# A post-norm decoder layer on one core: expert rounds moved into the cross attention steps, head pairs on 64-row tiles, split weights by way of DRAM

## The chip, the cores and the metric

The kernel runs on one core of one Trainium2 chip. The metric is the device time of one execution in microseconds. The kernel before has a median of 1275.68 us over 3 runs (1275.11 to 1279.91).

Five engines work side by side, each through its own queue of instructions in order: TensorE (PE; its weight loads are listed apart as PEld), VectorE (DVE), ScalarE (ACT), GpSimd (POOL) and SyncE (SP), which here only issues DMAs. They wait for each other by semaphores.

## The reference

One decoder layer on x (2048 rows of 256) with a context of 1601 rows of 256:

```python
x = layernorm(x + linear_attention(x))            # 8 heads of 64; softmax over features for q, over rows for k
# cross attention: 16 heads of 16
scores = einsum('bhqd,bhkd->bhqk', Q, K) * scale
out    = einsum('bhqk,bhkd->bhqd', softmax(scores), V)
x = layernorm(x + out @ Wo + bo)
# feed-forward: 16 experts of 128, the best 4 of each row weighted, and one shared network
act  = silu(x @ w1[e].T) * (x @ w3[e].T)
x = layernorm(x + sum_e combine[:, e] * (act @ w2[e].T) + shared(x))
```

The kernel computes all 16 experts for all rows and multiplies the hidden vector by the gate (0 where the expert was not chosen).

## The kernel before, in words

**Rows, chunks, groups, steps.** The 2048 rows are 4 chunks of 512. Cross attention goes through 16 groups (4 chunks times 4 groups of 4 heads), and a group through KT = 13 steps, one for each 128 keys: 208 steps. In a step PE makes four score tiles (`scores`, L755: one head, 128 keys by 512 rows, into banks 0 to 2 in turn), ACT takes the exponential of each (L538), and `weigh` (L766) multiplies them by the values, four heads side by side in four 32-column strips of the array.

**Row maxima.** The exponentials need the maximum of each row and head first. PE makes the scores a second time, with rows on partitions (`max_unit`, L733, 400 keys a unit, 64 units a group, three banks), and DVE reduces each unit (`read_max`, L1084). This runs 16 steps ahead of the steps that use it (LEAD); a stretch of 79 units comes before the first step. The negated maximum is turned (`turn_max`), copied by ACT (`copy_max`, L487) and written by DMA into the query stack (`stack_max`), so that the score product subtracts it.

**Precision.** Scores are bf16 products: queries and keys are each split into three bf16 parts, and six products of parts are stacked on 96 of the 128 rows. The experts' products are fp32r with two parts each (x_hi, x_lo, w_hi, w_lo), three products: `hidden` (L902 to L904) has 12 matmuls of 512 columns a network, `second` (L917 to L921) has 6.

**Order.** Four stages follow each other: linear attention and projections, which end in the split of keys (DVE L997 to L1002) and queries (L1073 to L1077); the 79 units; the 208 steps, into which the end of each earlier chunk (turn, output projection, layernorm, gate logits) is placed at fixed steps; and the 68 expert rounds (4 chunks times 17 networks, index i), in which ACT and POOL also split the weights for the first 17 (`first_part_w`, `second_part_w` L405). A round on DVE is `silu` (L1246), gate times inner product (L1252), their product (L1260) and its second part (L1265); on ACT it is tanh (L575) and the first part (L582). All four DVE operations of a round are on DVE alone.

POOL clears the value array and writes the rows of ones into the key stack (L384 to L388) once the context product is done, and computes the inverse deviations (L394). SP issues the DMAs in a fixed order.

## Time and profile before

| | |
|---|---|
| median of 3 runs | 1275.68 us |
| the profiled execution | 1280.25 us, span 1278.4 us |
| PE, DVE, ACT, POOL busy | 92%, 72%, 49%, 8% of the span |
| first score tile of the steps | 293.7 us |
| last value product of the steps | 952.2 us |
| granted TensorE clock, mean | 0.956 of full speed |

```profile
PE   6993887799999999999999999999989989999996
PEld 3471555422323333333333332333227768888885
DVE  1317786697888878788887888878427767677675
ACT  1210222105777776777767777677783432322222
```

Each digit is the busy share of a fortieth of the span (32 us), in tenths. The steps of cross attention are digits 10 to 29: PE, DVE and ACT are all busy. The rounds of the experts are the last 10: PE is full and ACT is at a third of what it was.

### The profile page before, as it was taken

The numbers are of one execution on the slowest core, as the hardware profiler recorded it, in microseconds if no ns is written. First come the engines' busy times: TensorE is split into PE (matmuls) and PEld (weight loads), VectorE is DVE, ScalarE is ACT, GpSimd is POOL, SyncE is SP. The second block draws the span as 40 slices with busy tenths as digits, with TensorE's granted clock in tenths as the row PEclk, the third lists the DMA queues.
The fourth block names the chain that finished last, engine by engine and source line by source line (L and its number), as shares of the span: only waits on it lengthen the run. The fifth ranks groups of instructions, "written<-read, shape, count | busy, mean of one in ns | idle before, by whom it ended". The sixth has DMA issues, their size and how long they took to land. (4 is left out here: it accounts for less than half of the span.)

```text
span 1278.4 us, 16160 instructions
## 1 busy us (share of the span) xinstructions
PE 1177.9 (92%) x5844; PEld 579.3 (45%) x5844; DVE 925.0 (72%) x1830; ACT 628.3 (49%) x1141; POOL 107.4 (8%) x94
## 2 busy tenths in 40 slices
PE   6993887799999999999999999999989989999996
PEld 3471555422323333333333332333227768888885
DVE  1317786697888878788887888878427767677675
ACT  1210222105777776777767777677783432322222
POOL 1213011500000000000000000000013410000000
PEclk9997898857999999999999999999999989999998
DMA  8000962102000000000000000000004411212120
GB/s 294 1 1 33 139 73 74 50 0 62 14 13 2 13 14 13 1 14 13 14 8 7 14 14 14 1 2 1 1 4 153 132 50 59 83 50 83 51 83 17
DMA packets 43055, 53.13 MB, mean 42 GB/s; under 512 B 4864, under 2 KB 31168, under 8 KB 42720
## 3 DMA queue, kind: packets, MB, share of 16 engines
q1 hardware_dynamic: 39104, 48.55, 14.4%
q10 hardware_dynamic: 3872, 3.56, 0.9%
q8 instruction: 46, 0.75, 0.2%
q14 instruction: 33, 0.27, 0.1%
HBM read 44.06 MB, written 7.83 MB: 41 GB/s over the span
## 5 line engine op out<-in xcount | busy, mean ns | idle before, releaser
L1084 DVE TENSOR_REDUCE mpart<-psum 128x1 f32<-128x400 f32 (+1 forms) x1024 | 522.9, 567 | 105.8 <-PE psum L733 101.4
L538 ACT ACTIVATE region<-psum 128x512 f32<-128x512 f32 (+1 forms) x832 | 450.2, 598 | 183.5 <-PE psum L755 182.3
L733 PE MATMUL psum<-region 96*128 96x400 bf16 (+1 forms) x1024 | 308.8, 352 | 8.7 <-DVE mpart L1084 5.6
L755 PE MATMUL psum<-region 99*128 99x512 bf16 (+1 forms) x832 | 285.0, 386 | 12.6 <-DMA region<-maxT 9.7
L766 PE MATMUL psum<-region 128*32 128x512 f32 (+1 forms) x1664 | 223.4, 609 | 0.7 <-ACT region L538 0.7
L755 PEld LDWEIGHTS psum<-region 99*128 99x128 bf16 (+1 forms) x832 | 80.6, 100 | 236.1 <-ACT region L538 186.8
L733 PEld LDWEIGHTS psum<-region 96*128 96x128 bf16 x1024 | 101.3, 99 | 181.2 <-DVE mpart L1084 132.8
L582 ACT ACTIVATE act_hi<-act_h 128x512 fp32r<-128x512 f32 x68 | 43.0, 632 | 176.0 <-DVE act_h L1260 176.0
L902 PE MATMUL psum<-x_hi,w_hi 128*128 128x512 f32 x272 | 109.9, 404 | 1.9 <-POOL w_lo L405 1.9
L903 PE MATMUL psum<-x_lo,w_hi 128*128 128x512 f32 x272 | 108.0, 397 | 0.0
L904 PE MATMUL psum<-x_hi,w_lo 128*128 128x512 f32 x272 | 108.0, 397 | 0.0
L394 POOL TENSOR_TENSOR rstd<-var_eps,half_neg 128x1 f32<-128x1 f32 (+1 forms) x24 | 18.4, 767 | 863.8 <-DVE var_eps L1139 752.0
L1265 DVE TENSOR_TENSOR act_lo<-act_h,act_hi 128x512 fp32r<-128x512 f32 x68 | 48.8, 718 | 47.5 <-ACT act_hi L582 47.5
L1246 DVE SCALAR_TENSOR_TENSOR silu_h<-tanh_h,psum 128x512 f32<-128x512 f32 x68 | 46.6, 685 | 41.9 <-ACT tanh_h L575 41.8
L917 PE MATMUL psum<-act_hi,w_hi 128*128 128x512 f32 x136 | 54.6, 402 | 8.8 <-ACT act_hi L582 8.7
L1260 DVE TENSOR_TENSOR act_h<-silu_h,weighted 128x512 f32<-128x512 f32 x68 | 56.7, 834 | 2.3
L902 PEld LDWEIGHTS psum<-x_hi,w_hi 128*128 128x128 f32 x272 | 51.7, 190 | 14.0 <-POOL w_lo L405 2.2
L766 PEld LDWEIGHTS psum<-region 128*32 128x32 f32 (+1 forms) x1664 | 32.8, 108 | 54.9 <-ACT region L538 40.3
L904 PEld LDWEIGHTS psum<-x_hi,w_lo 128*128 128x128 f32 x272 | 51.4, 189 | 12.5
L575 ACT ACTIVATE tanh_h<-psum 128x512 f32<-128x512 f32 x68 | 40.4, 593 | 33.5 <-PE psum L904 33.5
L903 PEld LDWEIGHTS psum<-x_lo,w_hi 128*128 128x128 f32 x272 | 51.6, 190 | 11.4
L918 PE MATMUL psum<-act_hi,w_lo 128*128 128x512 f32 x136 | 54.7, 402 | 0.0
(148 smaller groups left out, 1027.0 us busy)
## 6 DMA issues: line engine op xcount, KB each, us to landing
blend_a<-gates_d SPq DMA_DIRECT2D x32, 256.0 KB, 3.2
blend_b<-gates_d SPq DMA_DIRECT2D x32, 256.0 KB, 3.2
region<-qparts_d SPq DMA_DIRECT2D x96, 64.0 KB, 2.2
region<-kparts_d SPq DMA_DIRECT2D x6, 800.5 KB, 28.0
qparts_d<-region SPq DMA_DIRECT2D x4, 768.0 KB, 3.5
kparts_d<-region SPq DMA_DIRECT2D x3, 800.5 KB, 5.3
xT<-in_xT SPq DMA_DIRECT2D x1, 2048.0 KB, 8.9
x_sb<-in_x ACTq DMA_DIRECT2D x1, 2048.0 KB, 24.1
```

Source lines behind the costliest of these rows:

```text
L538: act.activation(prob[0:r, s % 3, j, :], bank(n % ST_BANKS)[0:r], ACT.Exp).then_inc(p_ready, 1)
L733: pe.matmul(bank(MAX_BANKS[u % len(MAX_BANKS)])[:, 0:w], qstack[0:SROWS, buffer(G), j, qt * P:(qt + 1) * P], kstack[0:SROWS, g * GROUP + j ...
L755: pe.matmul(bank(n % ST_BANKS)[0:r], kstack[0:SROWS + LEVELS, g * GROUP + j, kt * P:kt * P + r], qstack[0:SROWS + LEVELS, buffer(G), j, :] ...
L766: mm = pe.matmul(bank(4)[VW * j:VW * (j + 1)], vals[0:r, kt, g * GROUP + j, :], prob[0:r, s % 3, j, :], start=(kt == 0), stop=(kt == KT - 1))
L902: pe.matmul(out_bank, w_hi[:, e, col], x2_hi[tok], start=(k == 0), stop=False)
L903: pe.matmul(out_bank, w_hi[:, e, col], x2_lo[tok], start=False, stop=False)
L904: mm = pe.matmul(out_bank, w_lo[:, e, col], x2_hi[tok], start=False, stop=(k == DK - 1))
L917: pe.matmul(bank(6 + d), w_hi[:, e, cols[d]], act_hi[:, i % 2, :], start=(e == 0), stop=False)
L918: pe.matmul(bank(6 + d), w_lo[:, e, cols[d]], act_hi[:, i % 2, :], start=False, stop=False)
L1084: dve.tensor_reduce(mpart[:, u // UNITS % 2, v // PIECES, v % PIECES:v % PIECES + 1], bank(MAX_BANKS[u % len(MAX_BANKS)])[:, 0:w], X, ALU. ...
L1260: dve.tensor_tensor(act_h[:, i % 2, :], silu_h[:, :], weighted[:, :], ALU.mult).then_inc(act_ready, 1)
L1265: dve.tensor_tensor(act_lo[:, i % 2, :], act_h[:, i % 2, :], act_hi[:, i % 2, :].bitcast(F32), ALU.subtract).then_inc(act_lo_ready, 1)
```

## The change

1. `max_unit` and `scores` take fp32r operands. Queries and keys have two parts each and three products, on 48 rows; two heads lie in the two 64-row halves of the array (side 0 and side 1). One max unit is now 512 keys of two heads in two banks, and DVE reduces both in one instruction of 1024 elements; 26 units a group, two a step, and two of the 26 hold the last 66 keys of four row tiles (8 short matmuls). LEAD is 17 steps. The maximum is not split any more.
2. 42 of the 68 rounds run inside steps 67 to 192, a third in each step: `part_of_round` makes six of the first inner products ("first"), the six matmuls of the round before's output ("out"), or the six of the second inner product ("second"). One bank (2) holds the inner product, banks 6 and 7 the output; the score ring shrinks from three banks to two, and the max units from two pairs of banks to one. The other 26 rounds follow the steps.
3. In these 42 rounds `product` and `second_part_act` are on POOL, and ACT takes the first part and tanh of a round between the second and third exponential of its "first" step.
4. Everything that used bank 5 (turns, projection, logits, gates) takes a slot of the score ring and is copied out by ACT; ACT's waits follow the ring.
5. `weigh` comes two steps behind (s - 2) and ahead of the step's scores; from step 67 on, scores 0 and 1 are adjacent, and 2 and 3.
6. The weights are split at the start: POOL makes both parts of each of the 17 networks, SP stores them to DRAM, and each round loads its own (768 KB) by one DMA. SP issues this before it stores the key parts; POOL does it before it clears the value array, and now fills the whole key stack with ones before the key loads.

```diff
-SPLIT = 6
-LEVELS = 3
+SPLIT = 3
+LEVELS = 2
...
+IN_STEPS = 42
+FIRST_PIECE = KT * GROUPS + KT + 2
...
+        def unit_bank(u):
+            return (4, 6)[u % 2] if u < SINGLE else 4
+        def unit_free(u):
+            return u - 1 if u < SINGLE else u
...
+        def ring_bank(n):
+            return n % 3 if n < NARROW else (n - NARROW) % 2
...
+            load_raw(0)
+            for e in range(FFN):
+                if e + 1 < FFN:
+                    load_raw(e + 1)
+                store_split(e)
+
             sp.wait_ge(k_split, 1)
...
+            for e in range(FFN):
+                pool.wait_ge(ld_raw[e % 2], 16 * 3 * (e // 2 + 1))
+                if e >= 2:
+                    pool.wait_ge(split_written[e % 2], 16 * (e // 2))
+                link(pool.tensor_copy(w_stage[:, e % 2, 0, :], w_raw[e % 2]))
+                pool.tensor_tensor(w_stage[:, e % 2, 1, :], w_raw[e % 2], w_stage[:, e % 2, 0, :].bitcast(F32),
+                                   ALU.subtract).then_inc(raw_split, 1)
...
-            pool.memset(region1[SROWS:SROWS + LEVELS, 0:KW], 1.0 + 0x3F80 * 2.0 ** -23).then_inc(zeros_ready, 1)
+            pool.memset(kstack[:, :, :].bitcast(F32), 1.0).then_inc(zeros_ready, 1)
...
+            def product(r):
+                pool.wait_ge(weighted_ready, r + 1)
+                if r >= 1:
+                    pool.wait_ge(act_lo_ready, r)
+                pool.tensor_tensor(act_h[0], silu_h[:, :], weighted[:, :], ALU.mult).then_inc(act_ready, 1)
...
                for j in range(GROUP):
+                    if j == 2:
+                        if kt == 1 and G >= 1:
+                            copy_num(G - 1)
+                        r, part = piece(s)
+                        if part == "first":
+                            if r >= 1:
+                                first_part_act(r - 1)
+                            tanh(r)
...
             def max_unit(u):
...
+                    for side in range(SIDES):
+                        rows_of = slice(HALF * side, HALF * side + SROWS)
+                        mm = pe.matmul(bank(unit_bank(u) + side)[:, at * w:(at + 1) * w],
+                                       qstack[rows_of, buffer(G), p, t * P:(t + 1) * P],
+                                       kstack[rows_of, g * PAIRS + p, keys], start=True, stop=True)
...
+            def part_of_round(s):
+                r, part = piece(s)
+                if part == "first":
+                    if r == 0:
+                        pe.wait_ge(ring_read, NARROW)
+                    else:
+                        pe.wait_ge(weighted_ready, r)
+                    inner(r, 0, bank(H_BANK))
+                if part == "out" and r >= 1:
+                    outer(r - 1)
+                if part == "second":
+                    pe.wait_ge(silu_ready, r + 1)
+                    inner(r, 1, bank(H_BANK))
...
             for s in range(STEPS):                           # PE
+                if s >= 2:
+                    weigh(s - 2)
+                scores(s, 0)
+                if s >= FIRST_PIECE:
+                    scores(s, 1)
                 for u in units[0:1]:
                     max_unit(u)
+                part_of_round(s)
+                if s < FIRST_PIECE:
+                    scores(s, 1)
+                scores(s, 2)
+                if s >= FIRST_PIECE:
+                    scores(s, 3)
+                for u in units[1:]:
                     max_unit(u)
+                if s < FIRST_PIECE:
+                    scores(s, 3)
+                behind_scores(s)
...
+                for u in range(units_until(s - 1), units_until(s)):
+                    read_max(u)
+                    if u % UNITS == UNITS - 1:
+                        finish_max(u // UNITS)
+                r, part = piece(s)
+                if part == "first":
+                    silu(r)
+                if part == "second":
+                    weigh_inner(r)
```

## Rows read from the trace of the kernel before

**Rows 1.** Windows by stage: length; PE, PEld, DVE, ACT, POOL busy; clock; DMA share; GB/s.

```profile
294.00:910.00 616.00, 601.59 (x3498) 200.91 (x3496) 508.85 (x1101) 439.79 (x817) 10.72 (x9) 0.99 0.04 12
910.00:952.00 42.00, 36.74 (x207) 8.37 (x206) 9.10 (x40) 34.43 (x68) 0.00 (x0) 0.96 0.01 1
952.00:1031.00 79.00, 68.11 (x302) 53.01 (x299) 55.70 (x91) 32.06 (x53) 33.60 (x19) 0.95 0.41 120
1031.00:1278.00 247.00, 236.57 (x1028) 190.28 (x1026) 171.22 (x281) 71.39 (x121) 5.88 (x5) 0.98 0.19 60
```

**Rows 2.** Timeline of PE in one attention step: start, duration, what.

```profile
502.96 1.07 PE L766 MATMUL psum<-region 65*32 65x512 f32 x8
503.96 0.39 PE L755 MATMUL psum<-region 99*128 99x512 bf16 x1
504.19 0.68 PE L733 MATMUL psum<-region 96*128 96x400 bf16 x3
...
505.95 0.64 PE L766 MATMUL psum<-region 128*32 128x512 f32 x4
```

**Rows 3.** Groups by shape, 400 to 800 us: busy, mean ns; idle before.

```profile
L538 ACT ACTIVATE region<-psum 128x512 f32<-128x512 f32 x460 | 249.7, 599 | 106.1 <-PE psum L755 105.7
L1084 DVE TENSOR_REDUCE mpart<-psum 128x1 f32<-128x400 f32 x462 | 244.8, 567 | 52.8 <-PE psum L733 51.2
```

**Rows 4.** Timeline of PE and ACT in the last steps, where no maxima are left.

```profile
941.90 1.07 PE L766 MATMUL psum<-region 128*32 128x512 f32 x8
...
944.30 0.64 PE L766 MATMUL psum<-region 128*32 128x512 f32 x4
...
940.93 2.06 ACT L538 ACTIVATE region<-psum 128x512 f32<-128x512 f32 x4 [0.33 <-PE psum L755]
```

**Rows 5.** Timeline of PE in the expert rounds and at their end.

```profile
1035.40 0.62 PE L921 MATMUL psum<-act_lo,w_hi 128*128 128x512 f32 x2
1035.85 0.40 PE L902 MATMUL psum<-x_hi,w_hi 128*128 128x512 f32 x1
...
1039.58 0.62 PE L921 MATMUL psum<-act_lo,w_hi 128*128 128x512 f32 x2
...
1266.45 0.62 PE L921 MATMUL psum<-act_lo,w_hi 128*128 128x512 f32 x2
```

**Rows 6.** Groups by shape, 1040 to 1200 us, of DVE and ACT.

```profile
L1246 DVE SCALAR_TENSOR_TENSOR silu_h<-tanh_h,psum 128x512 f32<-128x512 f32 x38 | 26.1, 686 | 17.1 <-ACT tanh_h L575 17.1
L582 ACT ACTIVATE act_hi<-act_h 128x512 fp32r<-128x512 f32 x38 | 24.0, 632 | 92.6 <-DVE act_h L1260 92.6
```

**Rows 7.** Timeline of PE: gate logits and output projection of a chunk.

```profile
523.30 1.85 PE L822 MATMUL psum<-gate_wT,attnT 128*128 128x16 f32 x16
...
976.86 1.89 PE L800 MATMUL psum<-wo_c,attnT 128*128 128x256 f32 x8
```

**Rows 8.** GpSimd: timeline rows, and L400 from the groups of 400 to 800 us.

```profile
28.85 10.98 POOL L381 TENSOR_TENSOR x_sb<-x_sb,bo_row 128x256 f32<-128x256 f32 x16 [26.16 <-DMA gate_wT<-in_gateT]
97.96 10.77 POOL L388 MEMSET region<- 3x12808 f32 x1
965.73 1.83 POOL L405 TENSOR_TENSOR w_lo<-w_raw,w_hi 128x768 fp32r<-128x768 f32 x1 [4.79 <-ACT w_hi L522]
L400 POOL TENSOR_TENSOR x_lo<-attnT,x_hi 128x512 fp32r<-128x512 f32 x4 | 5.1, 1278 | 61.0 <-ACT x_hi L509 61.0
```

**Rows 9.** Timeline of DVE: first and second key part operation, and the next one.

```profile
100.61 8.97 DVE L997 TENSOR_SCALAR region<-region 128x1601 f32<-128x1601 f32 x1
...
110.65 1.82 DVE L999 TENSOR_TENSOR region<-region 128x1601 f32<-128x1601 f32 x1
...
132.12 0.69 DVE L1045 TENSOR_REDUCE small<-psum 128x8 f32<-128x512 f32 x1 [7.88 <-DMA kparts_d<-region]
```

**Rows 10.** DMA issues: count, KB each, us from issue to landing.

```profile
kparts_d<-region SPq DMA_DIRECT2D x3, 800.5 KB, 5.3
```

More of the change, by code:

```diff
@@ L61, in buffer @@
     return (G + 1) % GROUPS
[L64 to L70 removed]
+assert LASTK > 0 and REST * TPC <= CHUNK and UNITS == PER_STEP * KT
 def decoder_layer(nc, a, out):
@@ new lines, in ffn_copy_step @@
+        def ffn_copy_step(c):
+            step = FIRST_PIECE + 3 * FFN * (c + 1) + 2
+            return step if FFN * (c + 1) < IN_STEPS else None
+        EXTRA = {}
+        for group in range(CHUNKS * GROUPS - 1):
+            EXTRA[KT * group + TURN_MAX_AT] = ("max", group + 1)
+            EXTRA[KT * (group + 1) + 2] = ("num", group)
+        for c in range(CHUNKS - 1):
+            first = CHUNK_STEPS * (c + 1)
+            jobs = [(4, "attnT", 0), (5, "attnT", 1), (6, "proj", 0), (7, "proj", 1), (KT - 2, "x2T", 0),
+                    (KT - 1, "x2T", 1), (KT, "logits", 0), (KT + 4, "gate", 0)]
+            if ffn_copy_step(c) is not None:
+                jobs += [(ffn_copy_step(c) + 3 + half - first, "ffn", half) for half in range(2)]
+            for at, what, which in jobs:
+                assert first + at not in EXTRA
+                EXTRA[first + at] = (what, (c, which))
@@ new lines, in copy_ffn, with tanh @@
+                if c >= 1:
+                    if ffn_copy_step(c - 1) is not None:
+                        act.wait_ge(ring_full, extra_slot("ffn", (c - 1, 1)) + 1)
+                    else:
+                        act.wait_ge(ffnN_ready, 2)
+                for d in range(DK):
+                    act.activation(ffnT[:, d, :], bank(O_BANK + d), ACT.Copy).then_inc(ffn_copied, 1)
+            def tanh(r):
+                act.wait_ge(h1_ready, r + 1)
+                if r >= 1:
+                    act.wait_ge(silu_ready, before(r))
+                b = H_BANK if r < IN_STEPS else 2 * place(r)
+                act.activation(tanh_h[:, place(r), :], bank(b), ACT.Tanh, scale=0.5).then_inc(tanh_ready, 1)
@@ new lines, in outer @@
+            def outer(r):
+                c, i = divmod(r, FFN)
+                w_hi, w_lo = weights(r)
+                if r == 0:
+                    pe.wait_ge(max_read, SINGLE)
+                if i == 0 and c >= 1:
+                    pe.wait_ge(ffn_copied, DK * c)
+                pe.wait_ge(act_hi_ready, r + 1)
+                cols = [slice(2 * DK * HID + d * P, 2 * DK * HID + (d + 1) * P) for d in range(DK)]
+                for d in range(DK):
+                    pe.matmul(bank(O_BANK + d), w_hi[:, cols[d]], act_hi[place(r)], start=(i == 0), stop=False)
+                    pe.matmul(bank(O_BANK + d), w_lo[:, cols[d]], act_hi[place(r)], start=False, stop=False)
+                pe.wait_ge(act_lo_ready, r + 1)
+                for d in range(DK):
+                    mm = pe.matmul(bank(O_BANK + d), w_hi[:, cols[d]], act_lo[place(r)],
+                                   start=False, stop=(i == FFN - 1))
+                mm.then_inc(act_done, 1)
```

1235 lines of the change are left out of this document (697 added, 538 removed).

## The prediction

> **What bounds the kernel now.** I read the windows by stage first, then one step of each stage on the timeline. The attention steps take 616 us for steps 0 to 191 and 42 us for the last 16, the expert rounds 79 + 247 us [rows 1]. A round costs 4.18 us, 18 matmuls at 0.23 us with no gap [rows 5], so this stage is PE's. An attention step takes 2.99 us from one value product to the next; the value product holds PE 1.00 us, a score 0.23 us [rows 2]. Four scores and 4.9 units of 400 columns (about 0.17 us each, three recorded as 0.68 us with 0.34 us for the last to drain) give 2.7 us: PE is close to its limit, with about 0.3 us lost to handshakes. ACT and DVE are idle for 106 and 53 us of 400 there [rows 3]. With group and chunk ends a step averages 616 / 192 = 3.21 us; without maxima it is 2.40 us [rows 4]. So a round is moved from a stage where PE alone works to one where PE has little room: the matmuls stay on the bound engine, and the change gains only if the steps' own PE work shrinks, or waits get filled.
>
> **The terms.** All are made against the profiled span, 1278.4 us.
>
> Head, before the first score. The key split falls from 12 DVE operations to 4; the first half had cost 15 us with a first scale of 8.97 us while GpSimd filled the ones [rows 8, 9]. I put the split's end about 13 us earlier; its store grows from 2.4 to 3.2 MB, so the 7.9 us wait [rows 9] becomes 10.5. Against this stands SP's queue: the key store stands behind 17 weight stores, and these behind GpSimd. GpSimd is free at 39.8 us; a subtraction of 768 columns takes 1.83 us [rows 8], the copy I put at 1.3 us, between 0.7 and 1.8. With two slots and loads of 4 to 5 us a network takes 3.9 us (3.2 to 4.5), so the last is split at 106 us (94 to 116), just ahead of the keys at 111. If that cover is gone, each us more is a us lost. The fill of ones (10.8 us) then falls beside DVE's work from 112 us on and may hold one DVE operation for up to 8 us as it did before. Query split and first maxima: some 7 us less. Together -14 us, between -25 and +8.
>
> Steps 0 to 66. Before: 67 x 3.21 = 215 us. After, DVE has 24 reads of 1024 elements a group. I take 1.18 us each from 0.57 us for 400 [rows 3] at the same slope, so 2.3 us a step; ACT has 2.06 us [rows 4] plus 0.12; PE has 1.00 plus 8 matmuls, of which those on opposite halves may overlap: 5 to 8 times 0.23 gives 2.2 to 2.9 us. With 0.25 us of handshake I take 2.55 us, 171 in all, plus about 20 for ends of groups and of chunk 0: 191 us, -24.
>
> **Steps 67 to 192, the core.** Before: 125 x 3.21 + 2.6 = 404 us. After, PE has per step: value product 1.00, two score pairs and two unit pairs at 0.25 each if the halves overlap, six matmuls of a round 1.40, two more changes between the full array and halves 0.14 (the value product loses 0.15 to its two changes: 8 records of two passes of 512 columns in four strips are 0.85 us of streaming). That is 3.54 us. The short units are set by weight loads, 16 in 1.85 us [rows 7], so 0.9 us in place of 0.25 twice a group: 3.64 us on average, 10.9 us a round.
>
> Waits come on top. In the "second" step the last unit is read by DVE (1.2 us) ahead of `weigh_inner` (0.69), and PE's next "first" part waits for that: 0.6 us. Then the product on GpSimd (1.28 us, [rows 8]), the first part (0.63, [rows 6]) and tanh run in a row ahead of the third exponential; this ends 5.75 us into the step, and scores 0 and 1 of the next step need its bank in the ring of two: 0.8 us. A round is then 12.4 us; 42 are 521 us. Behind the delayed exponentials stand ACT's copies and the value product two steps on, which has slack. Twenty turns of groups take 0.6 us each plus 0.5 waiting for a ring bank: 22. Two chunk ends: 8 slots each, 8.4 us of PE (projection 1.89 each, logits 1.85, [rows 7]), 4 us of waiting, 6 us in which DVE is in norms and gate choice and PE waits at the next unit, since there is one pair of banks: 37. Two ends of expert chunks: 10. Sum 590 us, 4.68 a step: +186. From 490 (every wait filled) to 650.
>
> SP stands in order behind the round's waits; the 768 KB load is issued in the "out" step and needed two steps later, 7 us; a transfer of 800 KB took 5.3 us [rows 10]. I cost it at nothing; with the cover gone it is 1 to 2 us a round.
>
> Steps 193 to 207: two ring banks and no round. Score, exponential and 1.00 us of value product follow each other: 2.9 us (2.4 to 3.1) against 2.6: +5.
>
> **Tail.** Before 326 us. After: 26 rounds x 4.18 = 109, the end of chunk 3 on PE 9, one pair of turns 1, waits for DVE 6, last output 2, and from the last matmul to the end 11.5 as now (1266.9 to 1278.4, [rows 5]): 138.5, -188 (-195 to -175). The first 13 rounds had taken 75 us in place of 54, partly for weight splits that are gone.
>
> Sum: 1278.4 - 14 - 24 + 186 + 5 - 188 = 1243 us of span, 1245 with the 1.9 us around it, against 1280.25. The median of the kernel before is 0.9964 of that: **1241 us**, 2.7% less.
>
> **The row that carries it.** No row shows row tiles. The nearest is the value product, four column strips: one record of 256 columns over the full array takes 0.236 us (1.89 / 8, [rows 7]), so eight of 512 would take some 3.4 to 3.8 us one by one, and take 1.00 [rows 2]: strips overlap at 85% or better. For the two halves I take the same. The bounds are 0.23 and 0.47 us a pair.
>
> The Trainium skill, "TensorE: Matmul & The Clock Gate", Part 3, says that tiles in different row groups run side by side and measured 3.07 times for four; by it a pair would be between 0.23 and 0.30 us and the sum at most 25 us higher. Its "TensorEngine Tiling (Array Packing)", Key Properties, speaks against this change: a switch of tiling mode drains TensorE. The value product agrees in kind; a step now has four switches for two, and by a drain of twice what I take the sum would be 18 us higher.
>
> **Rivals.**
> - *The halves do not overlap.* Steps 67 to 192 get 0.88 us more PE work each, which fills some of the waits: 13.8 us a round, +57; steps 0 to 66 go to 3.1 us, +37. About 1334 us, slower by 4.6%. For: different halves are a form no row shows, and each score raises a semaphore and waits for its own bank, so pairs can come apart. Against: the strips. It decides once a mean step from 67 to 192 is above 4.96 us.
> - *DVE and PE in lockstep.* From step 67 a unit may only be written when the one before was read. DVE's other work (silu and `weigh_inner` 0.46 us a step, norms and gates another 0.5) then shows on PE. I count about 20 of 120 us; with half of it 1290 us, slower by 1.1%. For: DVE waits in order for tanh in "first" steps. Against: PE has 1.4 to 1.7 us of other work between two units.
> - *The waits are filled.* GpSimd and ACT finish in time, scores are not held: 1.4 us x 42 and half of the ends' waits go, about 1162 us. For: ACT is idle for 27% of 400 us now [rows 3]. Against: the chain through GpSimd above.
>
> **How the numbers follow.** Forecast 0.45 (1205 to 1275), waits filled 0.20 (1140 to 1205), lockstep 0.17 (1275 to 1310), no overlap 0.18 (1300 to 1350). The measurement tells 0.5% from no change, so 1269 to 1282 is "same". Faster: 0.42 + 0.20 = 0.62. Same: 0.03 + 0.05 = 0.08. Slower: 0.12 + 0.18 = 0.30. The range takes most of the outer cases and the head's bounds: 1165 to 1325.
>
> **What would show it.** Right: a score pair whose two matmuls start within 0.05 us and a pair period near 0.25; 12.4 us between "first" parts, with 0.6 and 0.8 us idle for `weigh_inner` and for the ring; steps 67 to 192 in 590 us; first score near 280; about 138 us after the last value product. Wrong: pairs 0.47 apart; PE waiting for reads of maxima in most steps; SP behind `act_done` with PE waiting for weights; or key stores that wait for GpSimd's splits.

## The result, and the profile after

| | before | after |
|---|---|---|
| median of 4 runs (range), us | 1277.8 (1275.1 to 1280.5) | 1291.3 (1288.3 to 1291.9) |
| span of the profiled execution, us | 1278.4 | 1289.7 |
| first score, us into the span | 293.7 | 266.7 |
| tail behind the attention steps, us | 326 | 136 |

The ratio is 1.0105, with a 95% interval of 1.0084 to 1.0126: the changed kernel is 1.05% slower, where 1241 us was forecast. Executions that are over 1.5% slower than the fastest of their kernel, at a lower granted clock, are left out of every ratio and of every difference below. The windows of the changed kernel by stage (columns as in [rows 1]), from the first units of maxima to the last value product:

```profile
229.00:267.00 38.00, 27.19 (x85) 11.20 (x85) 36.75 (x35) 0.59 (x1) 0.00 (x0) 0.54 0.06 19
267.00:476.00 209.00, 202.04 (x1212) 86.40 (x1211) 162.34 (x166) 150.80 (x293) 3.57 (x3) 0.92 0.06 18
476.00:1083.00 607.00, 556.11 (x3068) 269.36 (x3066) 390.59 (x489) 346.81 (x645) 114.85 (x90) 0.97 0.24 76
1083.00:1154.00 71.00, 58.85 (x205) 16.21 (x205) 0.85 (x3) 35.11 (x65) 1.27 (x1) 0.56 0.21 83
```

The stages against the forecast, whose total was 1243 us of span:

| stage | forecast | measured |
|---|---|---|
| head, to the first score | 280 | 267 |
| steps 0 to 66 | 191 | 209 |
| steps 67 to 192 (rounds inside) | 590 | 607 |
| steps 193 to 207 | 44 | 71 |
| tail | 138.5 | 136 |

The tail came as forecast. The miss of 46 us is -13 + 18 + 17 + 27 - 3, in four places. The windows are cut at the first matmul of a round, at 476 us; the value product that begins step 67 starts at 473.1 and that of step 193 at 1084.2. By the starts of steps, as all sums of steps below are made, it is 206 us for steps 0 to 66 and 611 for steps 67 to 192. The row of steps 193 to 207 shows the largest miss: a granted clock of 0.56, against 0.96 for the last steps in [rows 1].

One quiet step with a third of a round in it, TensorE's timeline (start, duration, what; "x2" is a head pair):

```profile
1054.64 1.06 PE L1034 MATMUL psum<-region 128*32 128x512 f32 x8
1055.63 0.50 PE L1023 MATMUL psum<-qstack,kstack 49*128 49x512 f32 x2
1056.03 0.50 PE L996 MATMUL psum<-kstack,qstack 48*128 48x512 f32 x2
1056.46 0.50 PE L1180 MATMUL psum<-x_hi,w_slots 128*128 128x512 f32 x1
...
1058.05 0.51 PE L1023 MATMUL psum<-qstack,kstack 49*128 49x512 f32 x2
1058.39 0.39 PE L996 MATMUL psum<-kstack,qstack 48*128 48x512 f32 x2
1058.71 0.64 PE L1034 MATMUL psum<-region 128*32 128x512 f32 x4
```

There is no gap. From start to start: value product 0.99 us, the pairs 0.40, 0.43, 0.34 and 0.32, six matmuls of the round 1.59, in all 4.07. The forecast for the same step was 3.54 and some waits. The two matmuls of a pair do run side by side (0.50 us recorded for both), but what follows starts 0.32 to 0.43 us after the pair, not 0.25. The weight loads of the pairs of this step, on TensorE's load engine:

```profile
1056.03 0.19 PEld L996 LDWEIGHTS psum<-kstack,qstack 48*128 48x128 f32 x2 [0.21 <-DVE mpart L1423]
...
1058.05 0.19 PEld L1023 LDWEIGHTS psum<-qstack,kstack 49*128 49x128 f32 x2 [0.36 <-issue]
1058.15 0.19 PEld L996 LDWEIGHTS psum<-kstack,qstack 48*128 48x128 f32 x2
```

At 1058.15 the load of a maxima pair runs while the score pair before it still streams, and the maxima pair starts 0.23 us after the start of its load. At 1058.05, behind a full-array matmul, load and matmul start in the same moment, so the load is not hidden. At 1056.03 the load waits for VectorE's read of the unit before, since there is one pair of maxima banks.

In a step without a round pairs also follow pairs with no change of form on either side (the changed kernel, TensorE; beside each of the first three a maxima matmul starts within 0.01 us):

```profile
298.12 0.50 PE L1023 MATMUL psum<-qstack,kstack 49*128 49x512 f32 x1
...
298.46 0.39 PE L1023 MATMUL psum<-qstack,kstack 49*128 49x512 f32 x1
...
298.69 0.40 PE L1023 MATMUL psum<-qstack,kstack 49*128 49x512 f32 x1
298.93 0.39 PE L996 MATMUL psum<-kstack,qstack 48*128 48x512 f32 x1
```

Here the second and the third pair are followed after 0.23 and 0.24 us, the time of a single full-array matmul; only the first, behind the value product, takes 0.34.

And behind the last piece:

```profile
1121.67 1.28 PE L1023 MATMUL psum<-qstack,kstack 49*128 49x512 f32 x2 [0.75 <-ACT region L813]
1122.88 1.93 PE L1034 MATMUL psum<-region 128*32 128x512 f32 x8
```

The value product takes 1.93 us in place of 1.06, and TensorE waits 0.75 us for ScalarE: 4.61 us a step, where [rows 4] had 2.40.

The gate choice of chunk 0, VectorE's timeline and then TensorE's (18 small rows in a line, of which the first stands here, and the read behind them):

```profile
480.94 0.21 DVE L1537 TENSOR_REDUCE small<-gate_work 128x4 f32<-128x64 f32 x1
...
485.43 1.22 DVE L1423 TENSOR_REDUCE mpart<-psum 128x2 f32<-128x1024 f32 x1
```

```profile
486.70 0.80 PE L996 MATMUL psum<-kstack,qstack 48*128 48x512 f32 x2 [3.15 <-DVE mpart L1423]
```

The maximum read stands behind 4.5 us of gate choice, and TensorE behind the read. What TensorE waited for in steps 67 to 192 in all (us in total, times, longest):

```profile
PE psum L996 <- DVE mpart L1423: 16.9, 11, 4.5
...
PE psum L1200 <- POOL act_lo_s L602: 4.6, 2, 3.4
...
PE psum L1180 <- issue: 3.1, 1, 3.1
```

These are waits at the ends of groups and chunks; in the quiet steps there are hardly any. The last row is one wait for weights, at 1005.0 us: SyncE issues in a fixed order, and that load stood behind the store of chunk 2's gates (995.9) and two loads of gate rows (997.5) until 998.3.

### The profile page after: what moved, and what is told of

It is laid out like the page before. It is cut to its first block, busy times and chain, and to the rows that moved or that the text cites. A ratio compares the mean times of both kernels' runs of the same rounds, so it can differ in the third digit from the quotient of the medians.

```text
span 1289.7 us, 15589 instructions
## 1 busy us (share of the span) xinstructions
PE 1158.0 (90%) x5844; PEld 595.9 (46%) x5844; DVE 793.1 (61%) x1076; ACT 621.4 (48%) x1152; POOL 228.8 (18%) x194
## 4 chain that ended last, share of the span: by engine, by line
PE 46%; issue 23%; DVE 12%; POOL 7%; ACT 6%; DMA 4%; ACTq 2%; SPq 1%; POOLq 0%; DVEq 0%
PE psum L1034 12%; PE psum L1023 11%; PE psum L996 4%; DVE mpart L1423 4%; ACT region L813 4%; PE psum L1180 3%; PE psum L1181 2%; PE psum L1182 2%; DMA tanh_h<-in_w2T 2%; POOL act_h_s L596 2%; POOL act_lo_s L602 2%; PE psum L1196 1%; POOL region L568 1%; PE psum L1200 1%; ACTq L635 1%
## 5 line engine op out<-in xcount | busy, mean ns | idle before, releaser
L1423 DVE TENSOR_REDUCE mpart<-psum 128x2 f32<-128x1024 f32 x384 | 461.6, 1223 | 232.0 <-PE psum L996 230.4
L1023 PE MATMUL psum<-qstack,kstack 49*128 49x512 f32 (+1 forms) x832 | 265.0, 508 | 14.2 <-ACT region L813 12.0
L996 PE MATMUL psum<-kstack,qstack 48*128 48x512 f32 (+1 forms) x1024 | 226.0, 420 | 29.1 <-DVE mpart L1423 28.0
L1023 PEld LDWEIGHTS psum<-qstack,kstack 49*128 49x128 f32 (+1 forms) x832 | 109.9, 192 | 290.9 <-ACT region L813 143.8
L996 PEld LDWEIGHTS psum<-kstack,qstack 48*128 48x128 f32 x1024 | 111.6, 199 | 66.7 <-DVE mpart L1423 60.7
L596 POOL TENSOR_TENSOR act_h_s<-silu_h,weighted 128x512 f32<-128x512 f32 x42 | 54.8, 1304 | 410.1 <-DVE weighted L1500 353.9
L1180 PE MATMUL psum<-x_hi,w_slots 128*128 128x512 f32 x168 | 76.6, 456 | 7.5 <-issue 3.1
L602 POOL TENSOR_TENSOR act_lo_s<-act_h_s,act_hi_s 128x512 fp32r<-128x512 f32 x42 | 53.6, 1276 | 106.7 <-ACT act_hi_s L764 106.7
L1181 PE MATMUL psum<-x_lo,w_slots 128*128 128x512 f32 x168 | 67.4, 401 | 0.0
L1182 PE MATMUL psum<-x_hi,w_slots 128*128 128x512 f32 x168 | 67.4, 401 | 0.0
L1500 DVE TENSOR_TENSOR weighted<-psum,rows 128x512 f32<-128x512 f32 x64 | 43.7, 683 | 9.4 <-PE psum L1182 5.5
```

What stands on the lines that cost most here:

```text
L596: pool.tensor_tensor(act_h[0], silu_h[:, :], weighted[:, :], ALU.mult).then_inc(act_ready, 1)
L602: pool.tensor_tensor(act_lo[0], act_h[0], act_hi[0].bitcast(F32), ALU.subtract).then_inc(act_lo_ready, 1)
L996: mm = pe.matmul(bank(unit_bank(u) + side)[:, at * w:(at + 1) * w], qstack[rows_of, buffer(G), p, t * P:(t + 1) * P], kstack[rows_of, g * ...
L1023: pe.matmul(ring(n)[0:r], kstack[rows, g * PAIRS + p, kt * P:kt * P + r], qstack[rows, buffer(G), p, :], start=True, stop=True).then_inc(r ...
L1180: pe.matmul(out_bank, w_hi[:, col], x2_hi[tok], start=(k == 0), stop=False)
L1181: pe.matmul(out_bank, w_hi[:, col], x2_lo[tok], start=False, stop=False)
```

## The experiments

Step times below are from the start of one value product to the next. Which kernel each builds on stands in its expectation. A time is the median beside that of the kernel before in the same series (1276.2 to 1277.1 us). Steps are read from one profiled execution of each kernel.

**The steps behind the last piece, and the clock.** Two ways to get rid of the 4.61 us.

e_shift:

```
-FIRST_PIECE = KT * GROUPS + KT + 2
+FIRST_PIECE = KT * GROUPS + KT + 17
```

> The 126 piece steps start 15 steps later (steps 82 to 207 in place of 67 to 192), and the first two blend rows of a chunk are loaded at its first round; everything is computed. Theory A (the 15 steps behind the last piece, 71 us in the changed kernel, are slow because TensorE's granted clock falls to half there; ahead of the first piece a step costs about 2.9 us with its ends): no step is left behind the last piece, 15 steps at 4.6 to 4.8 us become steps at 2.9 us, about 26 us less, near 1265. Rival B (the ring of two banks sets those steps whatever else runs in them, and the same waits come back inside the piece steps): less than 8 us of difference. Rival C (the later start moves chunk 0's blends and chunk ends onto each other): slower.

Measured: 1256.8 us, ratio 0.985 (0.982 to 0.987), 34.5 us less than the changed kernel. More than the 26 us of Theory A. Steps 67 to 81, which now have no round in them, fell from 72.3 to 47.4 us; steps 193 to 207 are 3.70 us each at full clock with pieces in them, but step 199 takes 12.2 us.

e_fill_trailing:

```
                 part_of_round(s)
+                if s >= FIRST_PIECE + 3 * IN_STEPS:
+                    filler(4, w_slots[:, 0, 0, 0:P], x2_hi[:, 0, 0, :], 3)
...
+                    filler(4, w_slots[:, 0, 0, 0:P], x2_hi[:, 0, 0, :], 2)
```

> Five matmuls of 512 columns over the full array, whose products nobody reads, are added to each of steps 193 to 207 (three between the score pairs, two behind them), 1.2 us of work at full clock. Theory A (half clock makes these steps 4.6 us): the granted clock stays near 1.0 and the steps fall to 3.1 to 3.5 us, in all 17 to 22 us less. Rival B (the handshake score, exponential, bank of the ring sets them): steps stay at 4.6 us, no difference. Rival C (work added is work paid): 15 x 1.2 = 18 us more.

Measured: 1279.9 us, ratio 1.0013, 11.4 us less than the changed kernel; Theory A had 17 to 22. The same stretch, 1100 to 1148 us, first of the changed kernel and then of this one:

```profile
1100.00:1148.00 48.00, 40.25 (x130) 11.46 (x126) 0.68 (x2) 22.31 (x41) 0.00 (x0) 0.50 0.07 29
```

```profile
1100.00:1148.00 48.00, 47.61 (x221) 20.35 (x218) 2.50 (x5) 26.19 (x48) 1.29 (x1) 1.00 0.17 67
```

More work, less time: the clock went from 0.50 to 1.00 and a step from 4.61 to 3.81 us. TensorE is now busy throughout, so the filler itself shows; whether fewer than five matmuls would have held the clock wasn't run. In the changed kernel the steps just ahead of the fall of the clock took 3.16 and 3.04 us, which is near the 2.9 forecast. At 3.1 us a step and with 2 us for the last two value products the stretch would take 48 of its 71 us, so 23 of the 27 us of miss are the clock's.

e_tail_loads removes the step of 12.2 us:

```
-                    for r in range(IN_STEPS, IN_STEPS + 6):
-                        load_weights(r)
+                if s >= KT * (CHUNKS * GROUPS - 1) and part == "second":
+                    load_weights(IN_STEPS + (s - KT * (CHUNKS * GROUPS - 1)) // 3)
```

> On top of e_shift: the six loads of 768 KB for the last rounds, which stood in SP's queue in one row at step 195, ahead of the slot loads of the rounds still to come, are issued one by one behind the second part of each round, from step 195 on. Theory A (in e_shift one step takes 12.2 us at 1081 us because TensorE waits 6.9 us for the weights of round 39, which stand behind six loads of about 4.2 us each): that step falls to 3.7 us, 7 to 8.5 us less than e_shift, about 1249. Rival B (the step waits for something else, or the tail then waits for its own weights): within 3 us of e_shift, or the tail grows by as much.

Measured: 1250.2 us, ratio 0.978 (0.975 to 0.981), 6.6 less than e_shift. In e_shift TensorE had started the part 6.92 us late, with six loads of 768 KB (3.57 us to issue all of them) ahead of the slot's load in SP's queue (issues of SP, then TensorE):

```profile
1070.31 3.57 SPq L465 DMA_DIRECT2D kstack<-wsplit_d  x6
1074.90 0.32 SPq L458 DMA_DIRECT2D w_slots<-wsplit_d  x1
```

```profile
1088.75 0.77 PE L1181 MATMUL psum<-x_hi,w_slots 128*128 128x512 f32 x1 [6.92 <-issue]
```

The same step is 3.70 us now. The forecast had put SP's queue at nothing. In the changed kernel the six loads come behind the last slot load and cost nothing; what SP's order does cost there is the wait of 3.1 us at 1005.0 us.

**What bounds a step with a third of a round in it.** Taking work away, adding work, taking the overlap away.

e_thin_parts leaves 14 of the 18 matmuls of each moved round out:

```
+                    if r < IN_STEPS:
+                        if k == 0:
+                            mm = pe.matmul(out_bank, w_hi[:, col], x2_hi[tok], start=True, stop=True)
+                        continue
```

> Left out: of the 18 matmuls of each of the 42 rounds inside steps, 14 (one matmul is left in each inner part and two in the outer part). Everything else, the other engines' work and all waits, stays. Theory A (TensorE bounds these steps; the full-array matmuls go at 0.23 us): 42 x 14 x 0.23 = 135 us less, down to where VectorE's 3.1 us a step (390 us in 126 steps) binds, so at least 90 us less. Rival B (handshakes between the engines set the 4.1 us of a quiet step): less than 60 us less. If it is more than 135, mode switches or the clock come on top.

Measured: 1293.0 us, 1.7 us more than the changed kernel (ratios 1.012 and 1.011, intervals overlapping); 135 us were taken away and nothing came back. Windows of this kernel: the whole stretch, and a piece of it:

```profile
476.00:1083.00 607.00, 553.42 (x2494) 207.83 (x2494) 391.05 (x489) 346.32 (x647) 115.36 (x91) 0.81 0.24 76
...
800.00:840.00 40.00, 37.26 (x201) 13.82 (x200) 28.78 (x32) 26.84 (x51) 8.92 (x7) 1.00 0.31 92
```

Over the stretch the clock is 0.81 in place of 0.97. Where it stayed at 1.00, a quiet step takes 3.64 us (value products at 804.69 and 808.33) in place of 4.07; where it fell to half, 5.1 to 5.5. So of 1.07 us of work taken away from a step 0.43 shows, and the clock takes that back.

e_parts_half_more adds two matmuls to each part (24 for 18 a round):

```
+                    if r < IN_STEPS:
+                        pe.matmul(out_bank, w_lo[:, col], x2_lo[tok], start=False, stop=False)
```

> On top of e_tail_loads: two matmuls are added to each of the 126 parts of rounds inside steps (24 in place of 18 a round; the products are added a second time or belong to no term, so the output is not the reference's). Theory A (at 4.1 us a quiet step TensorE's work is the bound): paid in full, 252 x 0.23 = 58 us more, 1303 to 1313. Rival B (handshakes still set the step and work fills them): less than 30 us more.

Measured: 1295.9 us, 45.7 us more than e_tail_loads for 58 us of work; Theory A is right for the quiet step and its time of 1303 to 1313 isn't reached. Quiet steps went from 4.07 to 4.51, which is all of the 0.46 added; at chunk ends part of it fills waits. So at 4.07 us TensorE's work sets the step, 0.4 us above a floor of about 3.65 that is there with little work too: more work is paid in full, less work is given back only down to the floor.

e_same_half lets both heads of a pair read the rows of side 0:

```
-                        rows_of = slice(HALF * side, HALF * side + SROWS)
+                        rows_of = slice(0, SROWS)
```

> Both heads of a pair read rows 0 to 48 (or 47) of the stacks, so the odd head's scores and maxima are those of the even one, and the two matmuls of a pair can't run side by side. Nothing else changes. Theory A (the halves overlap: a pair takes 0.33 us per 0.5 us recorded, against 0.47 for two of 0.23 one after another): four pairs a step cost 0.14 us more each or more, 126 steps x 0.56 = 70 us more in the piece steps, and less than that share in steps 0 to 66, where VectorE binds too: 1330 to 1370. If the weight load of the second matmul isn't hidden either (0.11 us each): 1370 to 1420. Rival B (the halves bring nothing, since a pair's 0.33 us is two weight loads and a start): within 10 us of the changed kernel.

Measured: ratio 1.170 (1.165 to 1.176), executions of 1487.6 and 1502.5 us, 204 more than the changed kernel and beyond both ranges of Theory A; the median of all four is 1522.8 us. A step at full clock, TensorE's timeline and one row of its weight loads:

```profile
704.25 0.73 PE L1023 MATMUL psum<-qstack,kstack 49*128 49x512 f32 x2
704.64 0.37 PEld L996 LDWEIGHTS psum<-kstack,qstack 48*128 48x128 f32 x2
704.82 0.63 PE L996 MATMUL psum<-kstack,qstack 48*128 48x512 f32 x2
705.38 0.50 PE L1180 MATMUL psum<-x_hi,w_slots 128*128 128x512 f32 x1
```

Two pairs take 1.13 us in place of 0.83 here, and 1.11 in place of 0.66 in the other half of the step; the step takes 4.82 in place of 4.07: the halves do overlap. Away from the changes of form the four matmuls on one half start 0.23 us apart. Start and length of the second of them:

```profile
704.59 0.39 PE L1023 MATMUL psum<-qstack,kstack 49*128 49x512 f32 x1
```

The next starts at 704.82 with weights whose load began at 704.64, on the same half and while the one before was still streaming. 0.75 us in each of 126 steps are 95 of the 204 us. The granted clock is lower too: its mean is 0.872 and 0.857 over these two executions and 0.926 in the changed kernel. Where it was low is known of the profiled execution alone (1543.2 us, mean 0.833): 0.50 from 267 to 400 us, although TensorE is busy all the time there. Neither theory had foreseen this part.

**What the places given up cost.** From the first piece on the score ring has two banks for three, and the maxima one pair of banks for two. Three kernels on top of e_tail_loads do this from step 26 on, with no piece there: steps 26 to 81 show the places without the work.

e_narrow_early, both places:

```
-        NARROW = slot(FIRST_PIECE, 0)
+        NARROW = slot(NARROW_STEP, 0)
...
-        SINGLE = units_until(FIRST_PIECE - 1)
+        SINGLE = units_until(NARROW_STEP - 1)
```

Where these kernels narrow the ring at step 26, they also take its order of scores from there: 0 and 1 adjacent, and 2 and 3.

> On top of e_tail_loads: the ring of three score banks becomes one of two, and the two pairs of maxima banks one, from step 26 on in place of step 82; no round's work is moved. Steps 26 to 81 thus run with the places that the rounds leave, but without rounds. Theory A (TensorE's work sets the steps, the places given up cost little as long as TensorE's other work fills the waits; alone they cost up to 1 us a step): a quiet step goes from 2.67 to 3.0 to 3.7 us at full clock, 56 steps, 20 to 55 us more. Rival B (the places are free): within 6 us. If the clock falls to half in these steps, 4.6 us a step and 100 us more, as in steps 193 to 207 of the changed kernel.

Measured: ratio 1.039 (1.033 to 1.045), executions of 1316.7 and 1334.9 us, some 75 us more than e_tail_loads; the median of all six is 1343.8 us. A quiet step at full clock:

```profile
366.08 1.07 PE L1039 MATMUL psum<-region 128*32 128x512 f32 x8
367.08 0.50 PE L1028 MATMUL psum<-qstack,kstack 49*128 49x512 f32 x2
367.48 0.50 PE L1001 MATMUL psum<-kstack,qstack 48*128 48x512 f32 x2
368.33 0.98 PE L1028 MATMUL psum<-qstack,kstack 49*128 49x512 f32 x2 [0.35 <-ACT region L818]
...
369.74 0.64 PE L1039 MATMUL psum<-region 128*32 128x512 f32 x4
```

It is 3.66 us, where the same steps with three banks take 2.67: the second score pair waits for the ring and comes apart (0.98 us). Where the clock is at half, as from 410 us on, a step is 5.13 us.

e_narrow_ring (NARROW and the order of scores moved) and e_narrow_units (only SINGLE moved, with the looser order of scores):

> As e_narrow_early, but only the ring of score banks is narrowed from three to two at step 26 (with its order of scores, pair by pair); the maxima keep two pairs of banks until step 82. Theory A (the ring is the place that costs: a score pair fills both banks, and the next waits for two exponentials of 0.55 us and a handshake): quiet steps stay near 3.65 us at full clock, and most of the 93 us of e_narrow_early remain, over 60. Rival B (the single pair of maxima banks costs it): quiet steps of 2.7 to 2.9 and less than 20 us more than e_tail_loads.

> As e_narrow_early, but only the maxima lose their second pair of banks at step 26; the ring keeps three banks and its order until step 82. Theory A (the ring costs): quiet steps 2.7 to 2.9 us, less than 20 us more than e_tail_loads. Rival B (the maxima banks cost: TensorE and VectorE, 1.23 us a read, take turns): 3.3 us or more a quiet step, over 40 us more.

Measured: ratio 1.027 (1.018 to 1.035), executions of 1302.0 and 1319.3 us (the median of all four is 1321.0), some 60 more than e_tail_loads, and 1381.2 us (1371.4 to 1388.9), 131 more. Quiet steps at full clock are 3.38 and 3.72 us, at half clock 5.04 and 5.56. Both expectations of a free place fell: either place alone costs 0.7 to 1.05 us a step, and they don't add up. The 0.7 us hold the order of scores as well; what the order does alone wasn't run. The pair of maxima banks weighs more. That its kernel is slower than the one that gives up both is the clock's doing: in steps 26 to 66 the mean granted clock is 0.58 there, 0.70 in e_narrow_early and 0.74 in e_narrow_ring. With one pair of maxima banks TensorE waits 1.10 us for the read:

```profile
510.59 0.50 PE L1001 MATMUL psum<-kstack,qstack 48*128 48x512 f32 x2 [1.10 <-DVE mpart L1428]
```

**Chunk ends.**

e_gates_spread cuts the gate choice into three parts:

```
-                    gate_choice(c - 1)
+                if c >= 1 and KT + 3 <= at <= KT + 5:
+                    gate_choice(c - 1, at - KT - 3)
```

> On top of e_tail_loads: the gate choice of a chunk, some 17 small VectorE operations in one row behind the maxima of one step, is cut into three parts in three steps, and its transpose and store come two steps later. Theory A (this row holds the next maximum read, TensorE idles 3 to 4.5 us for it and the clock falls for 5 to 8 us behind it, 5 to 8 us a chunk end): the idle stretches fall under 1 us and the time by 8 to 18 us against e_tail_loads. Rival B (VectorE's total work in those steps is what counts, wherever it stands): less than 3 us.

Measured: 1252.0 us, the same as e_tail_loads (ratios 0.980 and 0.978, intervals overlapping). Theory A fell. TensorE's waits for reads of maxima are 13.1 us where e_tail_loads has 11.3. It still waits 3.1 us once at the end of chunk 1, and two steps take 7.60 and 6.94 us. VectorE and GpSimd there:

```profile
711.77 1.29 POOL L600 TENSOR_TENSOR act_h_s<-silu_h,weighted 128x512 f32<-128x512 f32 x1 [11.56 <-DVE weighted L1504]
711.89 1.45 DVE L1448 TENSOR_TENSOR attn<-numN,den_rec 128x256 f32<-128x256 f32 x1
...
713.80 1.27 POOL L606 TENSOR_TENSOR act_lo_s<-act_h_s,act_hi_s 128x512 fp32r<-128x512 f32 x1 [0.74 <-ACT act_hi_s L768]
713.95 1.20 DVE L1563 TENSOR_TENSOR gate_work<-probs,top 128x64 f32<-128x64 f32 x1
```

The part that fell behind a "second" step met GpSimd's two operations, and a VectorE operation of 0.43 us took 1.45, one of 0.23 took 1.20, until GpSimd's ended. The Trainium skill, "SBUF — State Buffer", section "SBUF: two separate sides", says that VectorE and GpSimd share a pair of ports as an exclusive lock, and that the one that comes second stands still; it names VectorE operations such as these, with two inputs in SBUF, and the trace agrees. That the gain of Theory A went into these two stalls is argued: the spread choice without GpSimd's operations beside it wasn't run.

e_pool_order puts GpSimd's powers and token parts behind the round's work of the same step:

```
                 if part == "second":
                     product(r)
+                if c >= 1 and at == 8:
+                    inverse_deviation(c_var, c_rstd, c - 1, TPC)
```

> On top of e_tail_loads: in GpSimd's queue the powers for the norms and the second part of a chunk's tokens come behind the round's product or second part of the same step in place of ahead of it. Theory A (TensorE's waits of 3.4 and 1.2 us at each of two chunk ends for act_lo come from GpSimd, which waits in order for VectorE's variances and for ScalarE's token copy at the end of the step, ahead of the second part that TensorE needs): both waits go, 2 x 4.6 us, 6 to 9 us less. Rival B (VectorE and ScalarE come just as late, and the waits move to the next unit or score): less than 3 us.

Measured: 1239.0 us, ratio 0.971 (0.969 to 0.974), 11.2 less than e_tail_loads. In the profiles TensorE's waits for act_lo are gone and steps 104 to 131 fell from 143.6 to 137.1 us, steps 156 to 183 from 146.2 to 144.6. This is 8 us; the profiled executions differ by 7. The expectation counts the two waits at each of two chunk ends; the trace of e_tail_loads has them once, 3.4 and 1.2 us at the end of chunk 1.

e_product_dve moves the product and second part inside steps to VectorE:

> On top of e_pool_order: the product and the second part of the activations of the 42 rounds inside steps run on VectorE in place of GpSimd. Theory A (TensorE bounds the quiet steps and VectorE has over 1 us to spare in each): 42 x 1.3 us of VectorE work disappear beside TensorE, between 5 us less (VectorE's small operations are no longer held while GpSimd works) and 5 us more. Rival B (VectorE is the second bound, and every operation ahead of a maximum read shows): 20 to 50 us more.

Measured: 1238.9 us, no difference. VectorE went from 350 to 389 us busy of 550 and nothing came later: it has room, outside the gate choice.

**The head.**

e_q_five repeats the subtraction of the query split three times:

```
+                    for _ in range(3):
+                        link(dve.tensor_tensor(qpart[:, 1, :], qf, qpart[:, 0, :].bitcast(F32), ALU.subtract))
```

> The changed kernel with VectorE's split of each chunk's queries made of five operations of 1024 elements again in place of two (the subtraction is repeated three times; the result is the same). It tests where the head's unforecast gain came from: the stretch from the key store's landing to the last query part took 124 us before and 103 after. Theory A (VectorE bounds that stretch and the split was sized wrongly in the prediction): 12 operations of 1.2 us, 12 to 16 us more. Rival B (the gain came from transfers or GpSimd, which no longer stand against it): less than 4 us more.

Measured: 1310.9 us, 19.6 more than the changed kernel, over the 12 to 16 expected. VectorE's operations of 1024 elements ahead of the first score (count, busy, mean ns):

```profile
L1412 DVE TENSOR_TENSOR region<-region 128x1024 fp32r<-128x1024 f32 x12 | 17.1, 1428 | 0.4
```

The first value product is 23 us later for 17.1 us of work. This stretch is VectorE's, and its work there is paid at least in full; where the other 6 us come from wasn't traced.

e_fill_prologue and e_best add unread matmuls behind the first units of maxima, to e_tail_loads and to e_pool_order:

```
                 max_unit(u)
+                filler(2, kstack[:, 0, 0:P], kstack[:, 1, 0:CHUNK], 2)
```

> On top of e_tail_loads: two matmuls of 512 columns over the full array, whose products nobody reads, behind each of the 34 units of maxima ahead of the first score (37.6 us, 1.1 us a unit, granted clock 0.54 there and half in the first steps). Theory A (half clock makes the first three steps 4.1 us in place of 2.7 and the units slow to start): the clock stays at 1.0, VectorE's 1.23 us a unit still sets the pace, and 4 to 7 us go. Rival B (added work is paid: 34 x 0.46): 5 to 16 us more.

> e_pool_order with the two unread matmuls behind each unit of maxima ahead of the first score (e_fill_prologue). Theory: both gains add up, 3 us less than e_pool_order, 1238 to 1243 us, about 2.8% less than the kernel before.

Measured: 1246.9 us (ratio 0.975, e_tail_loads 0.978) and 1237.8 us (0.970, 0.968 to 0.972; e_pool_order 0.971). The clock ahead of the first score (229 to 267 us) goes from 0.51 to 1.00, and the first two steps from 4.07 and 3.83 to 2.61 and 2.67. The gain of 3 us is there in the profile (steps 2 to 66 in 196.7 for 199.5 us), but between the medians the intervals overlap, in both pairs. e_best is 3.0% faster than the kernel before and 4.1% faster than the changed one.

## Why the prediction was wrong

**The core, 590 us forecast, 607 measured (611 by the starts of steps).** Three of its terms were off, two of them against each other.
- *The changes of form.* The step that failed is the price of a change between the full array and the halves: two more of them were put at 0.07 us each. The overlap itself, which was to carry the forecast, was taken rightly. With no change of form beside it a pair takes 0.23 us, and 0.47 us on one half (e_same_half), which are the prediction's two bounds. Four pairs and six matmuls of a round at 0.23 are 2.30 us; the forecast had 2.54 for them with its changes, and measured are 3.08. So 0.78 us a step go for changes and the loads that stand behind them, in place of 0.24. At each change the first matmul behind it takes 0.34 us in place of 0.23, where its weight load starts with it and not ahead of it, and the last ahead of it takes 0.32 to 0.33. [rows 2] could not show the first of these: there the bf16 score behind the value product is followed after 0.23 us. The other 0.16 us are in the first half of the step, where the load of the maxima pair waits for VectorE's read (1056.03 us). The prediction had named a dearer drain as a possibility, with 18 us for twice its price. The Trainium skill, "TensorE: Matmul & The Clock Gate", Part 3, states beside the 3.07 times that I had read that weight loads pass running matmuls only where the row group differs. The trace does not agree: in e_same_half the load at 704.64 us passes a matmul on the same half, which started at 704.59, and the next matmul starts 0.23 us behind that one.
- *The waits.* The 0.6 and 0.8 us a round for `weigh_inner` and for the ring are nearly absent: TensorE's longer work covers them. The quiet round thus came to 12.2 to 12.4 us, as forecast, out of other terms. A group of 13 quiet steps took 56.1 us, or 4.31 a step; 126 of them are 543 us, and 521 + 22 for turns had been forecast. That is luck: 0.54 us too little for the work of each step, 1.4 us too much for the waits of each round of three steps. Only the timeline tells.
- *Chunk ends.* Over 4.31 a step, steps 104 to 131 cost 26 us and steps 156 to 183 cost 32; with 8 us for the end of chunk 0 in steps 67 to 81 that is 66, and 47 had been forecast. Missing were GpSimd's queue (4.6 us at the end of chunk 1, e_pool_order; the diff moves the round's product there, and what stands ahead of it waits for VectorE and ScalarE), SyncE's queue, put at nothing (3.1 us at the end of chunk 2), a choice of 4.5 us that stops a maximum read rather than running beside it, and the lower clock around the stops (0.97 and 0.96 over these steps, 1.00 between them).

**Steps 193 to 207, 44 forecast, 71 measured.** The step that failed was to let them run at the clock of [rows 4]. Their work without it was sized well (3.04 to 3.16 us against 2.9). With the ring of two TensorE pauses 0.74 to 0.75 us in each step, the granted clock goes to the lower level (1.2 GHz), and stays. The unread matmuls of e_fill_trailing fill the pauses and add work at once, so which of the two brings the clock back isn't shown.

**Steps 0 to 66, 191 forecast, 209 measured.** The quiet step is 2.67, not 2.55 us: 8 us. The first three with a value product run at half clock, 4 us more. The ends of groups and of chunk 0 cost 26 us over the quiet step, where 20 had been put down; 3 of them belong to step 67, whose value product starts at 473.1 us.

**Head, -14 forecast, -27 measured.** The term that was mis-sized is the query split. Before, it was five VectorE operations a chunk (the groups of the kernel before, 180 to 256 us; busy, mean ns; L1076 is as L1074 and L1077 as L1075):

```profile
L1074 DVE TENSOR_TENSOR region<-region 128x1024 f32<-128x1024 f32 x4 | 5.7, 1427 | 0.1
L1075 DVE CAST region<-region 128x1024 bf16<-128x1024 f32 x4 | 3.6, 896 | 0.1
L1073 DVE CAST region<-region 128x1024 bf16<-128x1024 f32 x4 | 3.0, 754 | 0.7 <-DMA qparts_d<-region 0.7
```

After, two are left:

```profile
L1411 DVE TENSOR_TENSOR region<-region 128x1024 fp32r<-128x1024 f32 x4 | 5.7, 1427 | 0.1
...
L1410 DVE CAST region<-region 128x1024 fp32r<-128x1024 f32 x4 | 3.0, 759 | 0.0
```

21.6 us became 8.7, 13 us less where "some 7" had been put down for this and the first maxima together; e_q_five shows that such work is paid in full. From VectorE's first operation of the query loop to the first score it is 20 us less in all; the other 7 weren't traced. The loop itself begins only 6.6 us earlier (125.55 against 132.12 in [rows 9]): the key split ends 12 us earlier, near the 13 forecast, but the store is waited for 13.6 us, not 10.5. Of these, 2 us are a sign that the prediction had named: the key store is issued at 114.0 us, behind the store of the last weights, whose split GpSimd ends at 113.6 us and not at 106, while the keys were ready at 112.0. The bound of -25 was passed.

**Tail, -188 forecast, -190 measured.** A quiet round takes 4.20 us there, as forecast, and from the last matmul to the end it is 9.1 us, where 11.5 had been put down. The other terms weren't taken apart.

**The rivals.** That the halves don't overlap: refuted (e_same_half). That the waits are filled: they were, but by dearer changes of form and not by time won. Lockstep of VectorE and TensorE, which stood at 1290 us: the time is right and the mechanism isn't, beside rounds; it is real in steps without one (3.72 us, e_narrow_units), and TensorE's work for the round covers it. VectorE can take 39 us more for nothing (e_product_dve), and the 16.9 us of waits for reads are 9.9 us of three gate choices (3.15, 2.31, 4.47) and 7 us spread over eight places.

**What it missed as a whole.** The gain was booked where a round leaves the tail (4.18 us), and its price was to be the round's work minus filled waits. The experiments give the account of one third of a round:

| | us |
|---|---|
| quiet step, three ring banks, two pairs of maxima banks | 2.67 |
| with the places given up, no work in it (e_narrow_early) | 3.66 |
| with four of 18 matmuls (e_thin_parts) | 3.64 |
| with the third of a round | 4.07 |
| with eight matmuls a third (e_parts_half_more) | 4.51 |
| a third of a round in the tail | 1.39 |

Of 1.4 us of work only 0.4 shows; the hiding works. But 1.0 us goes for the banks that it needs, with the order of scores that came with them, so a third costs 1.40 us inside a step and 1.39 outside. Over a whole group of 13 steps at full clock it is 36.6 us without rounds (steps 13 to 25 of e_pool_order) and 56.1 with them, 1.50 a step. Moving a round thus brings nothing in quiet steps and costs at chunk ends. What the changed kernel won, it won in the head and from its scores and maxima (2.99 to 2.67 us a quiet step), and it gave that back to the clock and the ends. How much faster a kernel with pairs and with all rounds in the tail would be wasn't run.

## What to carry to other kernels

Hiding work in an engine's waits has two prices, the work that shows and the buffers that it takes from its host; measure the second alone, by giving the buffers up early, before the work is moved. Removing work from TensorE can bring nothing when the clock falls with it (e_thin_parts), and a stretch that it leaves with short waits can run at half clock: look at the granted clock of each stage, and lay out moved work so that no light stretch is left behind it. Where two forms of matmul alternate, count the changes in the timeline and put matmuls of one form side by side. Before a product goes to an engine that stands in order, read what stands ahead of it in the same step.

## What the runs showed of the hardware

- Two matmuls of 512 columns on opposite 64-row halves, 48 or 49 rows each, start together. Away from changes of form such pairs follow each other at 0.23 us, matmuls on one half at 0.23 us each, and full-array matmuls at 0.23 us each. The first fp32r matmul or pair behind a change between full array and halves takes 0.34 us, the last ahead of one 0.32 to 0.33.
- A weight load of 128 columns (0.19 us recorded) ran while a matmul on the same half was streaming (e_same_half, 704.64 us).
- The granted clock was at half with TensorE recorded busy for 40 of 48 us (steps 193 to 207), and in the profiled execution of e_same_half (1543.2 us) with TensorE busy throughout (0.50 from 320 to 400 us, 80.0 of 80 us busy). Unread full-array matmuls brought it back to 1.00 in both places where they were put.
- A VectorE operation of 0.23 us took 1.20 us beside a GpSimd subtraction of 1.27 us.
